# Moving the projection remainders off VectorE, halving an output product, and spreading VectorE's side work in a four-stage kernel

## Time and profile before

| | |
|---|---|
| median of 3 runs | 1438.47 us (1436.85 to 1441.33) |
| the profiled execution | 1435.74 us, span 1434.0 us |
| granted TensorE clock, mean | 0.937 of full speed |
| busy: PE, PEld | 84%, 39% of the span |
| busy: DVE, ACT, POOL | 79%, 75%, 58% |

### The profile page before, as it was taken

How to read it: one execution, slowest core, us unless ns; L and a number is a source line. 1 busy time by engine, 2 the same in 40 slices (tenths; PEclk the granted TensorE clock), 3 DMA queues, 4 the chain that set the end, 5 groups by cost and what they waited for, 6 DMA issues and landing times. The chain is left out here.

```text
span 1434.0 us, 26470 instructions
## 1 busy us (share of the span) xinstructions
PE 1198.4 (84%) x8837; PEld 561.1 (39%) x8837; DVE 1126.1 (79%) x1923; ACT 1074.9 (75%) x1719; POOL 834.9 (58%) x812
## 2 busy tenths in 40 slices
PE   4489898989898989885875788776679999999998
PEld 3234343434343434332453223232234444444443
DVE  5678888888888888885976999999957776777653
ACT  2178878787878787774966889885467787778775
POOL 3034656565656565540001899899547777777776
PEclk8589999999999999997997899998889999999999
DMA  5341414141414141100004799888477768766884
GB/s 132 104 132 53 141 40 140 41 140 41 140 40 141 41 139 47 46 2 1 0 2 125 266 306 299 299 283 264 166 175 185 178 178 191 189 177 178 194 199 121
DMA packets 123690, 198.63 MB, mean 139 GB/s; under 512 B 24604, under 2 KB 60088, under 8 KB 123576
## 3 DMA queue, kind: packets, MB, share of 16 engines
q1 hardware_dynamic: 122136, 195.08, 47.8%
q10 hardware_dynamic: 1440, 2.10, 0.5%
HBM read 167.76 MB, written 28.84 MB: 137 GB/s over the span
## 5 line engine op out<-in xcount | busy, mean ns | idle before, releaser
L1071 DVE TENSOR_REDUCE bmax<-p1b 128x4 f32<-128x512 f32 x640 | 405.6, 685 | 82.6 <-PE p1b L777 78.0
L698 ACT ACTIVATE pT<-p2b 128x512 f32<-128x512 f32 x640 | 348.6, 598 | 92.0 <-PE p2b L830 90.3
L2220 POOL TENSOR_TENSOR hid_l<-e_hid,w_experts 128x1024 f16<-128x1024 f32 (+1 forms) x136 | 281.2, 2085 | 104.4 <-ACT w_experts L2355 103.5
L2454 DVE TENSOR_TENSOR e_hid<-ub,w_experts 128x1024 f32<-128x1024 f32 x128 | 155.8, 1223 | 121.4 <-ACT ub L2366 113.0
L648 POOL TENSOR_SCALAR_AFFINE_SELECT pT<-pT 128x512 f32<-128x512 f32 (+1 forms) x192 | 148.0, 787 | 164.4 <-ACT pT L698 164.4
L848 PE MATMUL ob<-pT,vs 128*32 128x384 f32 (+3 forms) x2048 | 187.4, 452 | 8.8 <-ACT o_sb L704 6.9
L1923 PE MATMUL yb<-ch,ident 128*128 128x512 f32 x256 | 135.1, 659 | 46.7 <-POOL ch L1893 46.5
L2355 ACT ACTIVATE w_experts<-e_hid 128x1024 f16<-128x1024 f32 (+1 forms) x136 | 139.4, 1025 | 38.0 <-DVE e_hid L2454 37.9
L2366 ACT ACTIVATE ub<-ub 128x1024 f32<-128x1024 f32 (+1 forms) x136 | 134.0, 985 | 37.9 <-PE ub L2271 36.1
L777 PE MATMUL p1b<-w_high 48*128 48x128 bf16 (+2 forms) x1792 | 130.0, 248 | 30.9 <-DVE bmax L1071 30.7
L830 PE MATMUL p2b<-w_high 50*128 50x512 bf16 (+3 forms) x1024 | 125.4, 302 | 2.7 <-ACT pT L698 2.1
(11 more groups left out here) (314 smaller groups left out, 2205.0 us busy)
## 6 DMA issues: line engine op xcount, KB each, us to landing
w_experts<-shares SPq DMA_DIRECT2D x256, 256.0 KB, 4.3
brow<-bc_rows SPq DMA_DIRECT2D x64, 512.0 KB, 4.0
crow<-bc_rows SPq DMA_DIRECT2D x64, 512.0 KB, 5.3
q_stacks<-w_low SPq DMA_DIRECT2D x96, 128.0 KB
k_stacks<-w_low SPq DMA_DIRECT2D x96, 128.0 KB
w_high<-q_stacks SPq DMA_DIRECT2D x128, 96.0 KB, 2.3
w_high<-k_stacks SPq DMA_DIRECT2D x128, 96.0 KB, 2.3
w_high<-nparts SPq DMA_DIRECT2D x128, 4.0 KB
```

Source lines behind the costliest of these rows:

```text
L698: act.activation(pT[:, g2 % 2, stored(u), :], p2b[bank_of(g2, u)][:, :], ACT.Exp, scale=SCALE).then_inc(exp_done, 1)
L1071: dve.tensor_reduce(to, bank, AX, ALU.max).then_inc(first_read, 1)
L2220: pool.tensor_tensor(flat(hid_l[:, rounded(p), 0:n, :]), flat(hid[:, place(p), 0:n, :]), rounded_half(p, 0, n), ALU.subtract).then_inc(spl ...
L2454: dve.tensor_tensor(h, u, flat(share[:, p % SHARES, :, :]), ALU.mult).then_inc(hid_ready, 1)
```

## The change

- Attention, remainders: ScalarE copies the projection a second time, in float32, from PSUM to SBUF (`projected`, which is the tile `gated`), right after the high part; this copy frees `auxb`. The first subtraction moves from VectorE to GpSimd and reads the copy. The middle part's rounding moves from unit 4 to unit 7.
- Attention, output product: its first two tiles are made in slot 7, the other two in slot 0 of the next round; gate and addition move to units 2 and 6 of slot 0. The normalisation moves from slot 0 to unit 4 of slot 7.
- Attention, order: the four value products go to slot 4 (late), 5 (early), 6 (early) and 6 (late). The square moves to unit 6 of slot 5, its sum to unit 9 of slot 5, the start of the root to unit 1 of slot 6, hT's copy to unit 3.
- Scan: ScalarE lays dt into PSUM (`lay_step`) at the end of a batch, VectorE multiplies it there by hT, after the last `run` and the residual instead of before them.
- Experts: the statistics go in five pieces to steps 11 to 15, and the loop on the chip becomes straight code.

```diff
-O_COPY_AT, HIGH_AT, MT_AT, HT_AT, MID_AT, NEG_COPY_AT, OT_AT, V_COPY_AT = 0, 0, (1, 3), 2, 4, 4, 6, 9
-RES_AT, NORM_AT = 3, 0
-SQ_AT = 4
-RC_AT, SUM_AT, START_AT, MERGE_AT = (3, 9), (5, 7), (5, 9), (6, 6)
+VALUE = {(4, "value_b"): 0, (5, "value_a"): 1, (6, "value_a"): 2, (6, "value_b"): 3}
+WO_FIRST, WO_LAST = (0, 1), (2, 3)
+O_COPY_AT, HIGH_AT, MT_AT, HT_AT, MID_AT, NEG_COPY_AT, OT_AT, V_COPY_AT = 0, 0, (1, 3), 3, 7, 4, 6, (2, 9)
+NORM_AT, GATE_AT, ADD_AT = 4, 2, 6
+SQ_AT = 6
+RC_AT, SUM_AT, START_AT, MERGE_AT = (3, 9), (5, 9), (6, 1), (6, 6)
...
 GpSimd, slot: after clear_future(... masked_last), ahead of the multiplies of slot 4
+                if prep and 1 <= g < 5:
+                    j, J = g - 1, (r + 1) * 4 + g - 1
+                    pool.wait_ge(aux_read, aux_use(r, g, "project") + 1)
+                    pool.wait_ge(hi_ready, J + 1)
+                    pool.wait_ge(split_ready, J + 1)
+                    pool.tensor_tensor(res, projected, parts[:, j % 2, 0, :], ALU.subtract).then_inc(res_ready, 1)
...
 ScalarE, slot, unit 0, after the copy of the high part
+                        act.wait_ge(res_ready, b * 4 + j)
+                        if r >= 2:
+                            act.wait_ge(post_done, r - 1)
+                        act.activation(projected, projection(r, g)[:, :], ACT.Copy).then_inc(aux_read, 1)
...
 TensorE, slot
                 pairs(0)
+                if g == 0:
+                    side("wo")
                 if 1 <= g < 5:
                     side("project")
+                if (g, "value_a") in VALUE:
+                    side("value_a")
...
                 pairs(4)
-                if 3 <= g < 7:
-                    side("value")
-                if g == GROUPS - 1:
-                    side("wo")
+                if (g, "value_b") in VALUE:
+                    side("value_b")
+                if g == GROUPS - 1 and post:
+                    if r == B:
+                        wo_first(range(TILES)).then_inc(aux_done, 1)
+                    else:
+                        wo_first(WO_FIRST)
...
 VectorE, round B, slot 0
+                        dve.wait_ge(post_done, B - 2)
+                        for n in range(B - 2):
+                            collect(dve, k, n)
+                        apply_gate(B, B - 2)
+                        add_gated(B, B - 2)
                         dve.wait_ge(post_done, B - 1)
-                        for n in range(B - 1):
-                            last = collect(dve, k, n)
+                        last = collect(dve, k, B - 2)
...
-                    if prep and u == RES_AT and 1 <= g < 5:
-                        j, J = g - 1, b * 4 + g - 1
-                        dve.wait_ge(hi_ready, J + 1)
-                        dve.wait_ge(split_ready, J + 1)
-                        dve.tensor_tensor(res, projection(r, g)[:, :], parts[:, j % 2, 0, :], ALU.subtract).then_inc(aux_read, 1)
...
 Scan
+    def lay_step(self, act, b):
+        act.wait_ge(self.dt_ready, b + 1)
+        act.activation(self.dtxb[:, :], self.dt[:, b % 2, :], ACT.Copy).then_inc(self.dt_laid, 1)
     def times_input(self, dve, b):
-        dve.tensor_tensor(self.dtxb[:, :], self.dt[:, b % 2, :], self.hT[:, b % 3, 1:S + 1], ALU.mult).then_inc(self.dtx_ready, 1)
+        dve.tensor_tensor(self.dtxb[:, :], self.dtxb[:, :], self.hT[:, b % 3, 1:S + 1], ALU.mult).then_inc(self.dtx_ready, 1)
...
 Experts
-            with eng.Fori(1, B - 2) as r:
+            for r in range(1, B - 2):
...
+                def next_stats(p):
+                    if p == 11:
+                        entry.stat_sums(dve, b + 1)
+                    elif p == 12:
+                        entry.stat_start(dve, b + 1)
+                    elif p > 12:
+                        entry.stat_newton(dve, b + 1, p - 13)
```

More of the change, by code:

```diff
@@ L476, in aux_of @@
     if g == 0:
-        kinds.append("turn_x")
+        kinds += ["turn_x", "wo"]
     if 1 <= g < 5:
         kinds.append("project")
-    if 3 <= g < 7:
-        kinds.append("value")
+    kinds += [kind for at, kind in VALUE if at == g]
     if g == GROUPS - 1:
-        kinds += ["turn_m0", "turn_m1", "wo"]
+        kinds += ["turn_m0", "turn_m1"]
     return sorted(kinds, key=AUX.get)
@@ L855, in slot @@
                 late = not isinstance(r, int) or r >= 0
+                after = r >= 2
                 def aux_free(kind):
@@ L919, in side @@
                     if kind == "wo":
-                        if not post:
+                        if not after:
                             return skip(kind)
-                        aux_free(kind)
-                        for i in range(TILES):
+                        for i in WO_LAST:
                             for c in range(2):
@@ L926, in side, with wo_first @@
                     mm.then_inc(aux_done, 1)
+                def wo_first(n):
+                    pe.wait_ge(aux_read, aux_use(r + 1, 0, "wo"))
+                    for i in n:
+                        for c in range(2):
+                            mm = pe.matmul(auxb[:, i * P:(i + 1) * P], mT[:, c, i * P:(i + 1) * P], k.wo[:, c, :], start=(c == 0), stop=(c == 1))
+                    return mm
                 if isinstance(r, int) and (r, g) == (B, F_TURN_AT):
@@ L1524, in step @@
                     front.copy_z(act, 1)
+                    front.lay_step(act, 0)
             rounds(act, step)
@@ L1719, in batch_stats, with stat_newton @@
         link(dve.tensor_scalar(self.var[:, :], self.stat[:, :, 1], EPS, None, ALU.add))
-        rsqrt_steps(dve, link, self.var[:, :], self.half[:, :], self.rstd[:, :], self.rtmp[:, :])
+        rsqrt_start(dve, link, self.var[:, :], self.half[:, :], self.rstd[:, :], self.rtmp[:, :])
+    def stat_newton(self, dve, b, n):
+        link = Chain(dve, self.dve_stats, b * STAT_LINKS + 6 + 3 * n).link
+        rsqrt_newton(dve, link, self.half[:, :], self.rstd[:, :], self.rtmp[:, :])
+    def batch_stats(self, dve, b):
+        self.stat_sums(dve, b)
+        self.stat_start(dve, b)
+        for n in range(3):
+            self.stat_newton(dve, b, n)
     def gates(self, dve):
@@ L2031, in step @@
                         entry.sigmoid(act, front.preb)
+                if back:
+                    act.wait_ge(dBx_ready, (r + 1) * PAIRS + 2)
+                    front.lay_step(act, r + 1)
             rounds(act, step)
@@ L2085, in step @@
                         entry.strike(dve)
-                    if back and m == PAIRS - 2:
-                        dve.wait_ge(dBx_ready, (r + 1) * PAIRS + 2)
+                    if back and m == PAIRS - 1:
                         front.times_input(dve, r + 1)
@@ L2462, in step @@
                                     f()
-                        if ahead and p == 12:
-                            next_stats()
+                        if ahead and p < PAIRS:
+                            next_stats(p)
                 else:
```

68 lines of the change are left out of this document (39 added, 29 removed).

## The result

The changed kernel takes 1449.54 us (median of 8 runs, 1444.21 to 1453.35) against 1437.49 us (8 runs) for the kernel before: ratio 1.0076, 95% interval 1.006 to 1.0093. It is slower by 0.76%; forecast were 1419 us and faster. The profiled execution of the changed kernel took 1452.72 us, span 1451.0 us, mean granted clock 0.935.

What follows compares the result with a forecast made beforehand. TensorE was taken to bound experts and attention, VectorE the scan. Profiled 1435.7 - 14 (experts) - 7.4 (scan) + 0.6 (before batch 0) + 1.5 (attention) = 1416.4; the median is 2.7 above: 1419 us, range 1404 to 1433.

Steps and rivals of the forecast that it cites:

- Attention, slots 1 to 5: Attention rounds: the late remainder delays SP's saves, loads and `nparts`; these slots take 43.9 us against 42.08, +1.8 a round.
- the slot keeps 8.05 to 8.1: Attention slot, timed from P, its first second-score product: ScalarE's copy only replaces TensorE's stop before `turn_neg`; length stays 8.05 to 8.1 us.
- The two latenesses cover each other: Attention: SP's late DMAs and GpSimd's late masks fall in the same slots and overlap, except after slot 4 (1.0 us).
- The third rival: Attention: SP's and the masks' latenesses add, 8 instead of 1.8 us a round; at half +22, 1441 us; chance 0.08.
- Slot 6: Attention: two value products and VectorE's earlier sum leave stops of 0.4 and 1.0 us; 9.3 instead of 10.80.
- Slots 7 and 0: Attention: split output product and moved normalisation; slot 7 9.8 instead of 10.36 us, slot 0 8.65 instead of 8.37.
- The tail: Attention's end: the gate of slot 0 behind 24 of 28 statistics (4.7 us) holds the shared bank: +1 us.
- End of the ffn: Ahead of scan batch 0, ScalarE's copy stands bare before VectorE's last work of the ffn: +0.6 us.
- Scan: dt times x read from PSUM takes 0.60 instead of 1.80 us; 1.05 saved in each of seven batches, 7.4 us.
- needed only 4 us later: Scan: ScalarE's copy and wait push its next exponentials by 1.3 us, harmless because VectorE needs them only later.
- Experts: Experts stage: statistics in five pieces remove TensorE's 13 stops, 14 us (upper bound 15.1); straight code costs nothing, bounds -2 and +3.
- The first rival: Experts: GpSimd holds the small VectorE pieces, so half of the 15 us comes back: 1426 us; chance 0.15.

Runs made afterwards that it cites:

- lay_moved: Kernel before with only the scan's and experts' parts, ScalarE's copy of dt moved behind the next batch's first two exponentials, batch 0 as before: 1426.59 us, ratio 0.9925.

## Why the prediction was wrong

The forecast for the profiled execution lies 36.3 us below the measured one. By the table of the stages 10.8 of them are in the rounds, 8.8 in the scan, 7.7 in the experts, 4.4 at the start, 2.9 in the ffn and 1.7 in the tail. That the change made the kernel slower is attention's part.

- **Attention, slots 1 to 5: this step failed.** It had +1.8 us for these slots, and they took +3.0 (45.04 instead of 43.9). Two terms were wrong. First, "the slot keeps 8.05 to 8.1": I gave ScalarE's added copy no price. The stop that I saw came as forecast (third pair at P + 3.65, I had 3.6), but a second one of 0.42 follows ahead of the next slot, and slot 1 takes 8.70. Second, the chain behind the remainder was right up to SP (the saves began 8.84 us behind the slot's start where I had 8.85, and `nparts` followed the loads at once), but I took `nparts` as the DMA that decides. What TensorE waits for are the stack loads ahead of it, needed by the first scores (12.9 us in nearly four rounds). The run with SP's loads first shows that the order of the queue is 9.2 us of the 12.8; as it puts both the loads and `nparts` back on time, it is the view of waits that names the loads. That slot 3 begins 17.40 us behind slot 1 where I had 17.35 is luck: slot 1 was longer and slot 2 shorter than forecast.
- **"The two latenesses cover each other":** not shown. With the loads late, the masks cost TensorE 1.1 us in four rounds, with the loads on time 5.9, which speaks for it. But curing the masks gained only some tenths a round at the same clock, and a run with the masks first and the loads late was not made. The third rival's 8 us a round are not there in any case; that its +22 us is near the 18.4 that attention lost in all (start, rounds and tail) is chance.
- **Slot 6** took 8.95 (forecast 9.3), and the number is luck. I expected it from the moved value products and VectorE's sum, with stops of 0.4 and 1.0. With these moves and VectorE's remainders the stops are 0.84 and 1.13, and the slot takes 9.9 at full clock and 11.4 where the clock falls. It is short in the changed kernel where the slots before it are long: only one stop, 0.77, is left, and the clock stays up.
- **Slots 7 and 0:** slot 7 took 10.04 (9.8). Slot 0 took 9.32 instead of 8.65: it lasts 9.32 in every version with the second half of the output product and 8.37 in every one without, so that half costs nearly its whole 1.0 us, and the gap that I had it fill was not to be had.
- **The tail** +2.7 instead of +1: the gate behind 4.7 us of statistics was the right place and the price too small; with the gate first the tail is 41.5.
- **End of the ffn** +3.5 instead of +0.6: I priced the copy (0.6) and not what it stands behind. VectorE waited 13.8 us for it instead of 6.1 for GpSimd's dt, because it comes last in ScalarE's ffn program, behind copies and table loads for batch 1; 4.1 us came back at the next wait. In `lay_moved` this is gone.
- **Scan** +1.4, or some -2 over all profiles, instead of -7.4: the 7.4 were saved on VectorE (7.5 measured). The sentence that failed is "needed only 4 us later". ScalarE's stop is 11.3 us in seven batches, not a push of 1.3, and the lead that it eats is needed some pairs later. With the copy moved the scan's mean is 269.6, 5 us below the old one: the term was mostly right, its place was not.
- **Experts** -6.3 instead of -14: TensorE's stops were the right term (with the save moved they nearly vanish, and the stage is 12.3 shorter than before), but I did not look for what is late next. It was the load behind SP's save. The straight code was not nothing: -3.6, beyond my bound of -2. The first rival, pieces held by GpSimd, is wrong: in sum the Newton steps took 20.8 us against 20.3 before.

## What to carry to other kernels

When a step moves to a later place, go down each in-order queue that it feeds, the DMA-issuing engine's above all, and ask of every entry behind it who needs that one first: the entry that decides may be another than the one you follow. A saved microsecond is worth looking for only together with the next thing that is late; here the statistics' stop and that of SP's save hid one another, and curing one alone showed a fraction of the gain. An entry that waits at the head of a queue belongs behind those that could already go. And before a difference of a few us between two profiles is given to an edit, compare them slot by slot with the granted clock beside each slot: one fall of the clock in a slot was as large here as several of the effects in question. When instructions are held, add up all lines of their group; the hold can move from one line to its neighbour.

## What was not expected of the hardware

- The same kernel with the same two stops (0.84 and 1.13 us) had TensorE's clock fall behind the second in some rounds and not in others; slot 6 then took 11.4 us instead of 9.9. With the old attention it was 10.8 instead of 9.25.
- A VectorE instruction on 4 elements took 2.02 us when GpSimd's 2.13 us instruction had begun 0.13 us before it, and the same instruction 0.16 in the next two Newton steps of that chain.
- Straight code in place of a loop on the chip shortened the experts by 3.6 us with the same instructions; TensorE's waits for VectorE fell from 12.9 to 10.3, its "issue" gaps from 2.1 to 1.3.
- Programs with the same beginning reached the first `qneg` between 64.3 and 67.3 us: a difference of 3 us there between two single profiles says little.
